# Context added by accumulating DMAs, and more probability chunks turned in blocks, in a gated cross-attention and quantised feed-forward kernel

## What is computed

```python
def _L0_xattn_ref(input1, input2, ...):        # input1: layer-normed x, input2: ctx; per batch 256 x 512
    theta_x = einsum('ld,bdt->btl', theta_w, input2) + theta_b
    phi_x = einsum('ld,bdt->blt', phi_w, input1) + phi_b
    scores = einsum('btl,bls->bts', theta_x, phi_x)
    p = softmax(scores, axis=-1)
    g_x = einsum('ld,bdt->btl', g_w, input1) + g_b
    t_x = einsum('bts,bsl->blt', p, g_x)
    h = relu(norm over (l, t) of t_x * ln_gamma + ln_beta)
    w_t = einsum('ol,blt->bot', out_w, h) + out_b
    return w_t + input2
...
x = x + tanh(g_xattn) * _L0_xattn_ref(layernorm(x), ctx, ...)
x = x + tanh(g_ffn) * ffn(layernorm(x))        # weights to -1, 0, 1; activations to 8 bits; 512 -> 2048 -> 512
```

## Time and profile before

| | |
|---|---|
| median of 3 runs | 297.99 us (297.82 to 298.01) |
| the profiled execution | 298.51 us |
| its span in the trace | 296.7 us |
| PE busy | 290.8 us, 98% |
| DVE, ACT, POOL busy | 81%, 66%, 67% |

### The profile page before, as it was taken

One profiled execution on the slowest core, in us unless ns is written; L12 is line 12 of the kernel. 1 busy time (PEld: TensorE's weight loads), 2 busy tenths in 40 slices (PEclk: granted clock), 3 DMA queues, 4 the chain that ended last, 5 costly groups with the idle time before them and its releaser, 6 DMA issues.

```text
span 296.7 us, 4393 instructions
## 1 busy us (share of the span) xinstructions
PE 290.8 (98%) x1310; PEld 155.9 (53%) x1310; DVE 239.7 (81%) x539; ACT 195.5 (66%) x319; POOL 198.3 (67%) x302
## 2 busy tenths in 40 slices
PE   8999999999999999999999999999999999999996
PEld 6766756575757565544444444444444444444444
DVE  3796977989898786999889787986986896867872
ACT  2387987989898898799765645465456456345620
POOL 3362598959593958657798777686786786655710
PEclk9999999999999999999999999999999999999999
DMA  7999596849494001010335474334343362641355
GB/s 238 408 418 411 227 325 259 263 147 344 155 345 146 0 2 35 1 39 0 71 71 59 88 142 106 61 82 106 72 96 84 75 103 72 131 116 29 83 100 180
DMA packets 56535, 42.23 MB, mean 142 GB/s; under 512 B 43456, under 2 KB 46656, under 8 KB 55488
## 3 DMA queue, kind: packets, MB, share of 16 engines
q1 hardware_dynamic: 56224, 41.69, 48.8%
q10 hardware_dynamic: 288, 0.27, 0.3%
HBM read 24.65 MB, written 6.82 MB: 106 GB/s over the span
## 4 chain that ended last, share of the span: by engine, by line
PE 79%; DVE 6%; POOL 4%; issue 3%; DMA 3%; ACT 2%; SPq 1%; POOLq 0%; DVEq 0%
PE bank L1240 37%; PE bank L1258 14%; PE bank L1184 8%; PE bank L1156 5%; PE bank L1201 4%; PE bank L1171 3%; PE bank L1133 2%; PE bank L1120 2%; DMA x<-x_dram 2%; PE bank L1143 2%; POOL stage L401 1%; PE bank L1271 1%; DMA probT<-prob 1%; POOL prob L385 1%; DVE xst L725 1%
## 5 line engine op out<-in xcount | busy, mean ns | idle before, releaser
L1240 PE MATMUL bank<-wq,stage 128*128 128x512 bf16 x512 | 113.3, 379 | 0.0
L1240 PEld LDWEIGHTS bank<-wq,stage 128*128 128x128 bf16 x512 | 50.1, 98 | 61.5 <-issue 2.3
L872 DVE SCALAR_TENSOR_TENSOR stage<-bank,s,stage 128x512 f32<-128x512 f32 x64 | 47.6, 744 | 22.6 <-PE bank L1240 18.6
L615 ACT ACTIVATE xn<-stage 128x1024 f32<-128x1024 f32 x31 | 32.8, 1057 | 46.1 <-DVE stage L872 46.1
L607 ACT ACTIVATE stage<-bank,s 128x512 f32<-128x512 f32 x64 | 43.1, 680 | 16.5 <-PE bank L1240 14.4
L1258 PE MATMUL bank<-wq,prob 128*128 128x512 bf16 x224 | 50.5, 379 | 0.0
L467 POOL TENSOR_SCALAR stage<-stage,hsc 128x1024 f32<-128x1024 f32 x30 | 33.3, 1119 | 20.6 <-DVE hsc L903 20.6
L877 DVE TENSOR_REDUCE m<-stage 128x1 f32<-128x1024 f32 x31 | 37.7, 1215 | 0.8
L1258 PEld LDWEIGHTS bank<-wq,prob 128*128 128x128 bf16 x224 | 21.9, 98 | 26.4
L1156 PE MATMUL bank<-ph,th 128*128 128x512 f32 x96 | 34.4, 471 | 0.3 <-DVE ph L753 0.3
L473 POOL TENSOR_SCALAR prob<-stage 128x1024 bf16<-128x1024 f32 x30 | 30.8, 1044 | 0.0
(11 more groups left out here) (122 smaller groups left out, 460.9 us busy)
## 6 DMA issues: line engine op xcount, KB each, us to landing
stage<-w1t_dram SPq DMA_DIRECT2D x4, 1024.0 KB, 12.1
stage<-w2t_dram SPq DMA_DIRECT2D x4, 1024.0 KB, 9.1
stage<-w3t_dram SPq DMA_DIRECT2D x4, 1024.0 KB, 6.5
x<-x_dram SPq DMA_DIRECT2D x7, 512.0 KB, 8.6
c_sb<-ctx_in_dram SPq DMA_DIRECT2D x7, 512.0 KB, 6.8
out_dram<-stage SPq DMA_DIRECT2D x14, 256.0 KB, 2.4
spill<-blocks SPq DMA_DIRECT2D x5, 512.0 KB, 2.6
placed<-spill SPq DMA_DIRECT2D x20, 128.0 KB, 2.8
```

Of the source, the lines that this page charges most:

```text
L615: A.activation(junk, h_sb[t % 2][:, half * HF:(half + 1) * HF], ACT.Square, accum_out=ssq[:, half:half + 1]).then_inc(sq_done, 1)
L872: V.scalar_tensor_tensor(h_sb[k][:, c * 512:(c + 1) * 512], up_banks(n)[1][:, :], s12[:, u % 2, 1, k:k + 1], sil[n % 3], ALU.mult, ALU.mul ...
L1240: last = mm(bank[:, :], turned[:, row:row + P], wq[:, at:at + 512], start=q == 0, stop=q == KI - 1)
```

## The change

1. For batches 2 to 7 `residual(i)` is gone from DVE. POOL issues `add_context(i)` right behind `gated_context(i)`: one DMA of 512 KB from `c_sb` to `x2` with an add at its destination, which increments a semaphore of its own (`xd_made`). `load_c(b)` from batch 4 on, `add_out(i, o)` from batch 2 on, and one `p_copy` wait for it.
2. `first_block(i)` gives the first chunk that goes in blocks: 2 for batches 1 and 6, 1 for batches 2 to 5, none for 0 and 7. So chunk 1 of batches 2 to 5 and chunks 2 and 3 of batch 6 leave TensorE and ACT for DVE and the DMAs.
3. `spill`, `blocks` and `placed` grow from two to three chunks; the move is split into `send_blocks` and `fetch_blocks`, and some loads change places in SP's list.
4. In ACT's table of weight work two entries of step 6 change places.

```diff
+        def first_block(i):
+            return 2 if i in (1, B - 2) else 1 if 2 <= i <= B - 3 else TC
...
-                if b >= 2:
+                if 2 <= b < 4:
                     sp.wait_ge(xc_made, 2 * (b - 1))
+                elif b >= 2:
+                    sp.wait_ge(xd_made[b - 2], 16)
...
+            def send_blocks(i):
+                n = TC - first_block(i)
+                sp.wait_ge(blocks_ready, block_no(i))
                 if i >= 2:
                     sp.wait_ge(blocks_moved, 64 * (i - 1))
+                sp.dma_start(spill[:, 0:TC * n * P], blocks[:, 0:TC * n * P]).then_inc(blocks_out, 16)
+            def fetch_blocks(i):
+                n = TC - first_block(i)
                 sp.wait_ge(blocks_out, 16 * i)
                 sp.wait_ge(tx_done, i)
                 for k in range(4):
...
+            def add_context(b):
+                pool.wait_ge(xn_ready, 2 * b + 2)
+                pool.wait_ge(cb_made, 2 * b + 2)
+                pool.dma_start(x2[:, 2 * b * T:2 * (b + 1) * T].rearrange("p (h t) -> p h t", h=DH), c_sb[:, b % 2],
+                               accum_op=ALU.add).then_inc(xd_made[b], 16)
...
                 gated_context(i)
+                if i >= 2:
+                    add_context(i)
...
-                6: ((M, 2, 4), (M, 2, 6), (S, 1, 0)),
+                6: ((M, 2, 4), (S, 1, 0), (M, 2, 6)),
...
                 add_out(i - 3, 1)
                 row_max(i, 0)
                 tx_var(i - 2)
-                residual(i)
                 row_max(i, 1)
...
-                if i >= 1:
+                if i >= 1 and first_block(i - 1) > 1:
                     turn_p(i - 1, 1)
...
                 scores(i, 3)
                 if whole:
                     values(i - 1, 3)
+                elif i == B - 1:
+                    values(i - 1, 2)
+                    values(i - 1, 3)
```

More of the change, by code:

```diff
@@ L78, in gated_cross_attention_bitffn @@
         probT = sb("probT", [P, 2, T])
[L80 to L83, removed]
+        blocks = sb("blocks", [P, TC * 3 * P])
+        placed = sb("placed", [P, TC * 3 * P])
+        spill = nc.dram_tensor("spill", [P, TC * 3 * P], F32, kind="Internal").ap()
         hn = sb("hn", [P, T])
@@ L153, in b_turn, with block_no @@
             return banks[2] if (i, c) == (B - 1, 2) else banks[4] if i == B - 1 and c == 3 else b_pt[c % 2]
+        def first_block(i):
+            return 2 if i in (1, B - 2) else 1 if 2 <= i <= B - 3 else TC
         def by_blocks(i):
-            return 1 <= i <= B - 3
+            return first_block(i) < TC
         def turn_no(i, c):
-            return c + (2 * i + 2 if by_blocks(i) else 0 if i == 0 else 2 * (B - 3) + 4 * (i - (B - 3)))
+            return c + sum(first_block(j) for j in range(i))
+        def block_no(i):
+            return sum(TC - first_block(j) for j in range(i + 1))
         def turned_p(i, c):
-            if by_blocks(i) and c >= 2:
-                return placed[:, :, (c - 2) * P:(c - 1) * P].rearrange("s q (c r) -> s q c r", c=TC)
+            if c >= first_block(i):
+                n = TC - first_block(i)
+                return placed[:, 0:TC * n * P].rearrange("s (q k c r) -> s k q c r", q=4, k=n, c=TC)[:, c - first_block(i)]
             return c_sb[:, 0, 0] if (i, c) == (B - 1, 2) else probT[:, 0] if i == B - 1 and c == 3 else probT[:, c % 2]
@@ L215, in gated_cross_attention_bitffn @@
         tail_q1_ready = sem("tail_q1_ready")
+        xd_made = {b: sem(f"xd_made{b}") for b in range(2, B)}
         blocks_ready, blocks_out, blocks_moved = sem("blocks_ready"), sem("blocks_out"), sem("blocks_moved")
@@ L257, in move_blocks @@
                 for k in range(4):
-                    sp.dma_start(placed[32 * k:32 * (k + 1)], spill_v[k]).then_inc(blocks_moved, 16)
+                    back = spill[:, k * n * P:(k + 1) * n * P].rearrange("(q b) r -> b q r", b=32)
+                    sp.dma_start(placed[32 * k:32 * (k + 1), 0:TC * n * P].rearrange("b (q r) -> b q r", q=4), back)\
+                        .then_inc(blocks_moved, 16)
             sp.dma_start(x2[:, 0:T], x_v[0][:, 0]).then_inc(xa_loaded, 16)
@@ L279, in _ @@
             load_x(4)
-            move_blocks(1)
+            send_blocks(1)
+            fetch_blocks(1)
             load_weight(1, 2)
             load_weight(1, 3)
+            load_c(4)
+            send_blocks(2)
             load_x(5)
-            load_c(4)
-            move_blocks(2)
+            fetch_blocks(2)
             load_x(6)
@@ L288, in _ @@
             load_c(5)
-            move_blocks(3)
+            send_blocks(3)
+            fetch_blocks(3)
             load_weight(2, 0)
@@ L292, in _ @@
             load_weight(2, 1)
-            move_blocks(4)
+            send_blocks(4)
+            fetch_blocks(4)
             load_weight(2, 2)
+            load_weight(2, 3)
             load_c(7)
-            load_weight(2, 3)
-            move_blocks(5)
+            send_blocks(5)
+            fetch_blocks(5)
+            send_blocks(6)
+            fetch_blocks(6)
             def turn_x(u):
@@ L637, in _ @@
                 if i >= 1:
-                    p_copy(i - 1, 0)
-                    p_copy(i - 1, 1)
+                    for c in range(min(first_block(i - 1), 2)):
+                        p_copy(i - 1, c)
                 if i >= 2:
@@ L771, in turn_blocks @@
                         dve.wait_ge(blocks_out, 16 * (i - 1))
-                V.transpose(blocks[:, :].rearrange("p (s k c r) -> p k c s r", s=4, k=2, c=TC)[:, k],
-                            prob[:, i % 2, :, (2 + k) * P:(3 + k) * P].rearrange("p c (s r) -> p c s r", r=32))\
+                V.transpose(blocks[:, 0:TC * n * P].rearrange("p (s k c r) -> p k c s r", s=4, k=n, c=TC)[:, c - first_block(i)],
+                            prob[:, i % 2, :, c * P:(c + 1) * P].rearrange("p c (s r) -> p c s r", r=32))\
                     .then_inc(blocks_ready, 1)
@@ L946, in third_step @@
                 low_part(2, th, b_th, 0, th_ready, thl_ready)
-                turn_blocks(1, 0)
-                turn_blocks(1, 1)
+                for c in range(first_block(1), TC):
+                    turn_blocks(1, c)
                 low_part(2, ph, b_ph, 1, ph_ready, phl_ready)
@@ L955, in third_step @@
                 tx_var(0)
-                residual(2)
                 row_max(2, 1)
@@ L979, in later_step @@
                     prep_mean(1)
-                if by_blocks(i - 1):
-                    turn_blocks(i - 1, 0)
-                    turn_blocks(i - 1, 1)
+                for c in range(first_block(i - 1), TC):
+                    turn_blocks(i - 1, c)
                 low_part(i, ph, b_ph, 1, ph_ready, phl_ready)
@@ L1284, in _ @@
                     weight_total({4: 1, 7: 2}[i], i)
-                if by_blocks(i - 2):
-                    values(i - 2, 2)
-                    values(i - 2, 3)
+                if i >= 2:
+                    for c in range(first_block(i - 2), TC):
+                        values(i - 2, c)
                 if i >= 3:
@@ L1316, in _ @@
                     values(i - 1, 2)
-                elif i >= 1:
+                elif i >= 1 and first_block(i - 1) > 1:
                     values(i - 1, 1)
```

21 lines of the change are left out of this document (12 added, 9 removed).

## The result

The changed kernel takes 302.23 us in the median of 4 runs (300.25 to 303.96), the kernel before 297.9 (297.81 to 298.01). The ratio is 1.0141 (95% interval 1.0107 to 1.0175): 1.4% slower, where 296.1 us and a gain were forecast. Its runs also lie 3.7 us apart, those of before 0.2 (0.8 to 1.7 in the sets of 15 to 31 runs of that kernel taken beside the experiments). The profiled execution is the fastest of the four, 300.25 us with a span of 298.4, so it shows the smallest of the losses: 1.7 us of span out of 4.3 us in the medians.

A forecast was written before the change was run, and what follows sets the result against it. PE, busy in 98% of the span, was taken as the bound. -2.69 - 0.2 + 0.6 + 0.4 = -1.9 us gave 296.1 us on the median's scale; 295.0 to 298.4 with 8 in 10.

The forecast's parts named there:

- PE's saving: Transposes of batches 2 to 5 and two sets of batch 6 leave PE: -2.69 us.
- Slacks of a middle step: Steps 4 to 6: later waits are covered, with 0.55 us left for x_norm; each step 0.44 us shorter.
- POOL's new instruction: Issuing the add from POOL takes 1 us (0.34 to 2.0), hidden in gaps where POOL waits for DVE.
- Step 3: PE's 0.6 us gap on batch 1's mean: third transpose +0.65, POOL's relief to -0.33; taken as -0.2 us.
- Step 7: Batch 6's two transposes delay DVE's chain to hn; PE's wait grows from 0.55 to 1.1-1.2 us: +0.6 us.
- The blocks' way: Block moves keep 2.8 us to spare, about 2 for batch 2; the add takes 2 us, so +0.4 us.
- The total: Sum of all terms: -1.9 us on the profiled execution's 298.51, giving 296.6, or 296.1 on the median's scale.
- Rival 1: Block moves of batches 2 to 5 arrive behind PE in every step because of the adds; 300.9 us, chance 0.17.
- Rivals 2 and 4: 2: POOL's issue delays x_norm, 297.0 or 300 us, chance 0.10; 4: better than forecast, 294.7 to 295.3, chance 0.10.
- rival 3: DVE, POOL and exp bound the steps, 297.5 to 298 us; sign: theta waits for ACT's exp; chance 0.13.

The follow-up runs named there:

- e5: The changed kernel with the context of batches 2, 4, 5 and 7 added by DMA, that of 3 and 6 by DVE; 297.79 us, ratio 0.9983.
- e3: The changed kernel with each adding DMA carrying 8 KB in place of 512 KB, most of the context left out of the sum; 297.22 us, ratio 0.9965.
- e1: The changed kernel with the context added by DVE again and no accumulating DMA, the larger block moves kept; 297.73 us, ratio 0.9994.
- e11: The changed kernel with one 1 MB weight load moved in SP's list behind the write of batch 5's blocks; 304.21 us, ratio 1.0184.
- e8: As e1 (context added by DVE), but batch 6 turned wholly by TensorE as before; 297.68 us, ratio 0.9989.
- e6: The changed kernel with only the context of batches 3 and 6 added by DMA, the others by DVE; 300.87 us, ratio 1.0096.
- e4: The changed kernel with POOL's DMAs copying the context over x rather than adding it, same bytes; 298.64 us, ratio 1.0038.

## Why the prediction was wrong

- **PE's saving** (-2.69 us): right. 24 transposes are gone, the steps 5 and 6 last 13.97 us as predicted with 13.98.
- **Slacks of a middle step**: right. `x_norm`, the first exp, and DVE's third transpose make PE wait nowhere in steps 5 and 6; the power takes 0.55 us in each step beside 0.94 to 1.53 in the earlier trace rows. The Trainium skill, "SBUF — State Buffer", "Who interferes with whom", has it that a DVE instruction with two SBUF inputs contends with a GpSimd instruction that reads SBUF. The trace agrees, and e5 shows it within one kernel: 0.55 us where the context is added by DMA, 0.93 and 0.94 in steps 3 and 6, where DVE adds it.
- **POOL's new instruction** (1 us, hidden): right, 0.92 to 1.07 us, with 0.56 to 0.60 of waiting ahead of it, and e3 shows that it costs nothing.
- **Step 3** (-0.2): right in sign; theta of step 4 starts at 53.34, against 54.90 before. From theta to theta step 3 is 1.68 us shorter; 1.30 of it are the transposes and `values` that left it, so 0.38 came on top where 0.2 was put.
- **Step 7** (+0.6 for DVE's chain): masked in the changed kernel by the wait for `placed` ahead of it. In e1, where it can be seen, the waits for `var_mm`'s input, `hn` and relu are 0.3, 0.4 and 0.7 us, 1.3 to 1.4 in all against 0.55 before: +0.8 where +0.6 was put. The relu was not among the terms.
- **The blocks' way** (+0.4): this is the step that failed. It gave the move 2.8 us to spare in the middle steps and about 2 for batch 2, and the add beside it 2 us; PE waited 5.2 us. For batch 2 both terms were mis-sized. In e3, with hardly any bytes in the add, the write took 4.2 us rather than 3.3 and the last read 4.2 rather than 3.2, so the blocks were there at 56.8 and PE came at 56.9: nothing to spare. The add's bytes then cost 3.1 us rather than 2: the four reads took 2.67 us to issue rather than 1.75, and the last landed after 6.5 us, at 59.9, where PE would have begun at 57.05. For batch 5 the term that failed is the write alone, 7.8 us where 3.3 was put. The sum had nothing for the weight loads, which stand ahead of it on the same engines and which the slower moves and the changed list had made late (both issued from 83.46, the first at 79.67 before). Here the add's bytes are not the cause of the slow write: it took 7.9 in e3, 5.3 in e1, and 4.2 in e11 with the add there and one weight load put behind it. The load was judged by one window of 2 us around the write (0.65 in the earlier trace rows) in which no big load was under way; the stretch from 46 to 98 us was at 0.66 as a whole, and both halves of the change add to it.
- **The total**: -1.9 us were forecast on the profiled execution's scale, +1.7 measured. The blocks' way alone is 4.8 us off; some of it comes back because the two waits of the earlier trace rows are gone. That the medians are 4.3 us apart and not 1.7 is in no term: the lower clock of three of the four runs was not thought of.
- **Rival 1** came true, in other places: not in each of four steps, but in two, and on the timed runs' scale dearer than its 300.9. Its reason against (idle share beside the write) was the error. The Trainium skill, "DMA: Bandwidth & Descriptors", "Issuing engines are not separate DMA queues", has DMAs of all issuing engines interleave on the same 16. The runs agree: the add is issued by POOL and the reads by SP, and with the add's bytes beside them the reads took 5.7 us rather than 3.6. Rivals 2 and 4 did not occur. Of rival 3 the outcome of e1 and e8, no or hardly any gain, had the size but another reason: single waits, not a period. One of them is its own sign, theta waiting for ACT's exp, in one step.

What stays open: how much of the 1.4% falls on step 4, on step 7 and on the clock in the timed runs, which have no trace; what in step 7 follows from the add of batch 6, since e6 has that add and no wait there; and whether another order of the loads would let e3's gain of 0.35% be had with real adds.

## What to carry to other kernels

Before work is given to DMAs, find for each transfer that an engine waits for what else is under way from its issue to its landing, the loads issued before it included, and take the spare time from that very step. A sum of the engines' share over the whole stretch is a warning when it comes near 1 (here 0.66 + 0.16 + 0.26), but it does not tell which kernel loses: four adds at 0.94 cost nothing, two at 0.88 came with 2.8 us of waits for `placed`. Two changes that are each free can cost 1.4% together when they draw on the same resource. And in a hand-written DMA list every wait and every large load delays all that stands behind it, so a transfer's slack is that of the list, not its own.

Before a wait in a table is given to a step, look up when it happens: a wait of 0.7 us at the start of this kernel was taken for one in step 7, and a version was built on it.

## What the runs showed of the hardware

An accumulating DMA between two places in SBUF held the engines 2.1 times as long as a plain copy of the same bytes (5.8% of the span in the changed kernel, 2.8% in e4, for 3.15 MB). In the stretch from 52 to 58 us the engines were at a share of 1.03 to 1.12 with only 225 to 232 GB/s moved. This is not the adds' doing alone. The kernel before, which has none, moved 241 GB/s at 1.00 from 52 to 54 us and 414 at 1.00 from 42 to 44 us, so a full share says little of the bytes.

An add of 8 KB took 5.6 us to land in the median beside other traffic (e3), in 144 packets like one of 512 KB, and 2.2 us in step 7, where little else was under way. TensorE's clock fell from 1.00 to 0.50 in e11 at 103 us, after PE had been idle for the 2.15 us up to 101.59, and was back at 1.00 at 107; in the changed kernel it stayed at 1.00 through a wait of 2.93 us.
